# A four-part graph network on one core: set-up without table round trips, a first layer on full-width rows, and work of the second layer moved into its edge loop

## Chip, cores and metric

The kernel is written in Bass for one NeuronCore of a Trainium2 chip, with the instruction stream and the semaphores of each engine written out by hand. The metric is device time in microseconds (us) of one execution. TensorE is called PE, VectorE DVE, ScalarE ACT, GpSimd POOL and SyncE SP, as in the profile.

## The reference, cut to what matters

There are 6,250 nodes with 128 features and 106,250 directed edges, sorted by destination. Four graph blocks follow one another, each with a residual sum and a layer norm. The change touches the first block and what prepares it:

```python
def _sage_conv(h, src, dst, n_nodes, Wl, bl, Wr):
    msg = jnp.take(h, src, axis=0)
    agg = jax.ops.segment_sum(msg, dst, num_segments=n_nodes)
    cnt = jax.ops.segment_sum(jnp.ones_like(src, dtype=h.dtype), dst, num_segments=n_nodes)
    agg = agg / jnp.clip(cnt, 1.0)[:, None]
    return agg @ Wl + bl + h @ Wr

h = _sage_conv(x, src, dst, n, Wl0, bl0, Wr0)      # 128 -> 256
h = _batchnorm(jax.nn.relu(h), g0, b0)
h = _sage_conv(h, src, dst, n, Wl1, bl1, Wr1)      # 256 -> 256
h = _batchnorm(jax.nn.relu(h), g1, b1)
return jax.nn.relu(h @ Wp + bp)                    # 256 -> 128
```

The three later blocks (Moebius, equivariant, graph attention) read the same edges. They use a list of nodes sorted by degree, and per-edge weights and scores that the loops of the first block compute on the side.

## The kernel before, in words

Nodes are padded to 49 tiles of 128 (`TILES`), edges lie in 831 blocks of 128. A **step** is one pair of an edge block and a node tile that it reaches: 880 steps (`STEPS`), taken as 110 bodies (`BODIES`) of 8 steps (`U`).

`setup` finds, for each node, where its edges begin (`ptr`), from that the list of steps, and a sort of the nodes by degree. It goes through DRAM tables: 49 gathers of destination rows (`drow`, L336), a table `ptr_tab` written and read back, then `stepT`/`stepE` written and read back, then 14 gathers of the steps' edge rows (L343). It also splits `x` in three bf16 parts whose sum is the fp32 value and writes them as the table `x_split` (L403 to L406). At its end it ranks the nodes (L451 to L466).

`sage_layer` runs twice (layer 0, layer 1). In a step:
- POOL gathers the 128 source rows with one indirect DMA (L700), from `x_split` in layer 0 (three parts of 128 columns) or `y_split` in layer 1 (three parts of 256). There are 16 slots (`SLOTS`), so POOL can be 12 to 16 steps ahead of PE.
- DVE makes the one-hot matrix edge-to-node of four steps at once (L200, bf16), into one of two halves.
- PE multiplies rows by one-hot, three bf16 matmuls (layer 0) or six (layer 1) (L789), into a ring of four PSUM banks.
- DVE adds the bank to `agg`, which lies feature by node (L884).

In each body PE and ACT also compute edge weights of the later blocks in fp32: L798 (256 columns), L808 (two of 256), and in layer 0 L802 (128 columns) and L815 (32 columns). DVE copies small pieces (L903, L908, L913), and ACT stores and loads (L727 to L745).

When the loop of a layer ends, `agg` is scaled by the reciprocal degree (L921), multiplied by `Wl` and added to the layer's own part times `Wr` (L829, L831; 14 chunks of 448 nodes, 2 halves of features), passed through relu (L757), tallied for the batch norm (L937) and normalised (L950). Layer 0 then transposes the result back to rows and splits it in three bf16 parts (L768, L957, L770, L959), which SP writes to `y_split` (L669); POOL meanwhile scatters the sorted node list (L704, 49 scatters). Layer 1 multiplies by `Wp` and adds the bias with a one-row matmul (L844, L845), adds `x` (L962), and runs a layer norm over 7 groups of 7 tiles (L503 to L519); POOL reduces the largest degree and gathers the first sources of each node (L1009, 49 gathers). The Moebius block starts with 49 gathers (L1104).

PE, ACT and DVE run the bodies in hardware loops of four (`fours`); POOL's stream is written out in full.

## Time and profile before

| | |
|---|---|
| median of 3 runs | 7617.18 us (7613.0 to 7625.78) |
| the profiled execution: its own time | 7613.21 us |
| its span, first to last instruction | 7611.2 us |
| granted TensorE clock, mean | 0.632 of full |
| set-up, until the first gather of layer 0 | 326.7 us |
| gathers of layer 0, first to last start | 326.7 to 1462.0 us |
| gathers of layer 1, first to last start | 1594.9 to 2709.3 us |
| first gather of the Moebius block | 2981.5 us |

A row of the timeline gives start, duration, engine, line, operation, what is written and read, and in brackets how long the engine had been idle and what released it. An fp32 matmul shows as two instructions ("x2"), each with a weight load of its own (engine PEld). "issue" is time in which the engine waited for nothing that the profile shows. The granted clock has two levels here, 0.5 (1.2 GHz) and 1.0 (2.4 GHz); a value between is a mean over time.

### The profile page before, as it was taken

Reading aid. Unit: us, or ns where it says so; the run is one execution under the profiler, and the core shown is the slowest. Engines: PE = TensorE matmul, PEld = TensorE weight load, DVE = VectorE, ACT = ScalarE, POOL = GpSimd, SP = SyncE. Lnnn points to the kernel's source line nnn. Section 1 sums busy time; section 2 is a strip of 40 time slices with the busy share of each in tenths; the row PEclk is TensorE's granted clock in tenths of the full one; section 3 lists DMA queues with packets and bytes.
Section 4 is the critical chain, followed back from the end, with each engine's and each line's share of the span. In section 5 each row is a group of like instructions: output and inputs, shape, how many; then the busy total and the mean of one; then the engine's idle time right before and its main releaser. Section 6 shows DMA issues by size and latency. Waiting matters only on the chain. (4 is left out here: it accounts for less than half of the span.)

```text
span 7611.2 us, 86798 instructions
## 1 busy us (share of the span) xinstructions
PE 2675.4 (35%) x13121; PEld 1768.7 (23%) x13121; DVE 4112.7 (54%) x10643; ACT 1491.7 (20%) x5205; POOL 5148.9 (68%) x5017
## 2 busy tenths in 40 slices
PE   0466666756677673000000005666667100000000
PEld 0244444435455442000000003333335100000000
DVE  5344443454444433676677866777777414444465
ACT  0000000120000010121222104777774000000000
POOL 3277777757777742777777564777774477777765
PEclk9666555667777775555555557788878555555555
DMA  2544444356666621222222113333332322222211
GB/s 36 101 126 123 126 123 125 88 171 198 197 198 198 195 62 45 49 46 48 48 47 48 35 26 95 101 101 101 101 101 56 84 55 52 52 52 52 53 39 32
DMA packets 433517, 681.95 MB, mean 90 GB/s; under 512 B 159150, under 2 KB 266608, under 8 KB 433120
## 3 DMA queue, kind: packets, MB, share of 16 engines
q0 software_dynamic: 203280, 470.84, 24.5%
q10 hardware_dynamic: 127152, 159.46, 6.3%
q1 hardware_dynamic: 102944, 50.32, 2.9%
q14 instruction: 120, 0.98, 0.0%
q8 instruction: 21, 0.34, 0.0%
HBM read 584.78 MB, written 95.44 MB: 89 GB/s over the span
## 5 line engine op out<-in xcount | busy, mean ns | idle before, releaser
L1116 POOL DMA_INDIRECT mb_rows<-x_tab,mb_idx x906 | 1009.1, 1114 | 342.5 <-issue 276.4
L789 PE MATMUL ps<-onehot,rows 128*128 128x128 bf16 x7920 | 945.4, 272 | 732.7 <-DMA rows<-x_split,srcS 329.5
L884 DVE TENSOR_TENSOR agg<-agg,ps 128x128 f32 (+1 forms) x1760 | 623.7, 354 | 954.6 <-PE ps L789 806.3
L1414 POOL DMA_INDIRECT eq_frow<-f_tab,srcS x880 | 894.6, 1017 | 356.8 <-issue 267.9
L1732 POOL DMA_INDIRECT gt_rows<-h_tab,gt_idx x906 | 931.8, 1028 | 298.7 <-issue 273.9
L700 POOL DMA_INDIRECT rows<-x_split,srcS x880 | 864.8, 983 | 379.3 <-issue 244.9
L700 POOL DMA_INDIRECT rows<-y_split,srcS x880 | 840.6, 955 | 333.2 <-issue 245.8
L1436 ACT ACTIVATE eq_pb<-eq_wrow 128x64 f32<-128x64 f32 (+1 forms) x3520 | 864.1, 334 | 430.9 <-DVE eq_msg L1553 366.7
L1476 PE MATMUL eq_ps<-eq_msg,eq_onehot 128*128 128x320 f32 x1760 | 739.6, 581 | 435.2 <-DVE eq_onehot L200 423.8
L789 PEld LDWEIGHTS ps<-onehot,rows 128*128 128x128 bf16 x7920 | 631.6, 120 | 1106.2 <-DVE agg L884 738.9
L1464 PE MATMUL eq_ps<-ident,eq_x 128*128 128x128 f32 x49 | 14.0, 291 | 1686.9 <-DMA eq_m<-in_L_gnn_W_l_D 1686.9
L1476 PEld LDWEIGHTS eq_ps<-eq_msg,eq_onehot 128*128 128x128 f32 x1760 | 425.9, 254 | 748.4 <-DVE eq_acc L1561 570.7
L200 DVE TENSOR_TENSOR onehot<-iota,dstS 128x512 bf16<-128x512 f32 x440 | 305.3, 694 | 275.3 <-issue 263.0
L1561 DVE TENSOR_TENSOR eq_acc<-eq_acc,eq_ps 128x320 f32 x880 | 425.0, 483 | 51.6 <-issue 29.8
L808 PE MATMUL ps<-w2d,hT 128*128 128x256 f32 x880 | 415.8, 624 | 0.0
L1464 PEld LDWEIGHTS eq_ps<-ident,eq_x 128*128 128x128 f32 x49 | 7.3, 151 | 1688.7 <-issue 1687.2
L731 ACT ACTIVATE wrow<-ps 128x512 f32<-128x512 f32 x220 | 131.3, 597 | 1268.7 <-PE ps L808 1268.7
L1845 DVE TENSOR_TENSOR gt_alpha<-gt_rows,gt_scores_in 128x196 f32<-128x196 f32 (+5 forms) x36 | 9.5, 264 | 671.5 <-DMA gt_rows<-h_tab,gt_idx 671.0
L1179 DVE TENSOR_TENSOR mb_prod<-mb_rows,mb_xd 128x256 f32<-128x256 f32 (+4 forms) x128 | 140.5, 1098 | 401.8 <-DMA mb_rows<-x_tab,mb_idx 322.3
L1153 ACT ACTIVATE mb_rows<-mb_rows,mb_gm 128x128 f32<-128x128 f32 x906 | 268.5, 386 | 361.6 <-DVE mb_gm L1222 361.6
L1009 POOL DMA_INDIRECT span_src<-in_src,span_at x147 | 161.0, 1095 | 243.3 <-DVEq L1805 158.5
L1548 DVE TENSOR_TENSOR eq_msg<-eq_pb,eq_frow 128x512 f32<-128x512 f32 x220 | 152.4, 693 | 259.5 <-DMA eq_frow<-f_tab,srcS 248.2
(395 smaller groups left out, 5021.9 us busy)
## 6 DMA issues: line engine op xcount, KB each, us to landing
eq_wrow<-w_tab ACTq DMA_DIRECT2D x223, 264.0 KB, 3.0
w_tab<-wrow ACTq DMA_DIRECT2D x220, 264.0 KB, 2.7
es<-in_side ACTq DMA_DIRECT2D x220, 136.0 KB, 2.6
mb_rows<-x_tab,mb_idx POOLq DMA_INDIRECT x906, 2.6
gt_rows<-h_tab,gt_idx POOLq DMA_INDIRECT x906, 2.5
rows<-x_split,srcS POOLq DMA_INDIRECT x880, 2.7
rows<-y_split,srcS POOLq DMA_INDIRECT x880, 3.1
eq_frow<-f_tab,srcS POOLq DMA_INDIRECT x880, 2.6
```

What stands on the lines that cost most here:

```text
L200: return dve.tensor_tensor(onehot[:, 4 * half:4 * half + 4], broadcast(s["iota"][:], four, 1), broadcast(s["dstS"][:, bass.ds(4 * b, 4)], ...
L700: pool.indirect_dma_start(rows[:, n % SLOTS, :], None, table, bass.IndirectOffsetOnAxis(ap=s["srcS"][:, n:n + 1], axis=0)).then_inc(gather ...
L789: last = pe.matmul(ps[:, u % 4, f * P:(f + 1) * P], rows[:, slot, at:at + P], onehot[:, u], start=(part == 0), stop=(part == 2))
L808: last = pe.matmul(ps[:, 7, 2 * n * P:(2 * n + 2) * P], hT[:, n * P:(n + 1) * P], w2d[:], start=True, stop=True)
L884: dve.tensor_tensor(into, into, ps[:, u % 4, 0:W].rearrange("p (k n) -> p k n", n=P), ALU.add).then_inc(added, 1)
L1116: pool.indirect_dma_start(rows[:, r, n, :], None, t["x1"], bass.IndirectOffsetOnAxis(ap=idx[:, r, n:n + 1], axis=0)).then_inc(gathered[r][ ...
L1153: act.activation(rows[:, r, n, 0:D], rows[:, r, n, 0:D], ACT.Copy, scale=gm[:, n:n + 1]).then_inc(scaled_ready, 1 if n + 1 < UPTO[p] else ...
L1414: pool.indirect_dma_start(frow[:, n % SLOTS, :], None, t["f"], bass.IndirectOffsetOnAxis(ap=s["srcS"][:, n:n + 1], axis=0)).then_inc(gathe ...
L1436: last = act.activation(pb[:, r % 2, u, f].rearrange("p c w -> p (c w)"), wrow[:, r, bass.ds(at, 1), lo:lo + 64].rearrange("p o f -> p (o ...
L1476: pe.matmul(ps[:, 4 * r + u, 0:MC], onehot[:, 4 * r + u], msg[:, r, u], start=True, stop=True).then_inc(step_done, 1)
L1561: dve.tensor_tensor(into, into, ps[:, 4 * (r % 2) + u, 0:MC], ALU.add).then_inc(added, 1)
L1732: pool.indirect_dma_start(rows[:, r, n, :], None, t["h"], bass.IndirectOffsetOnAxis(ap=idx[:, r, n:n + 1], axis=0)).then_inc(gathered[r][g ...
```

## The change

The last three quarters of the kernel are as they were. What is new:

- **Set-up.** No tables, no gathers, no split of `x`, no ranking. A new input `first` holds the destination of the first edge of each block. It is spread over the partitions; one compare with a count on DVE gives for each node tile how many blocks start before it; a bf16 one-hot product with ones gives the node tile of each step. The edge rows of the steps are then picked by 22 fp32 matmuls of 224 columns with selection matrices that DVE builds.
- **First layer** (`sage_first`). POOL gathers plain fp32 rows of `x` (512 bytes). The one-hot is fp32. PE runs two fp32 matmuls a step: one-hot by a column of ones (one column, counts degrees) and rows by one-hot (128 columns). DVE adds 129 columns. In bodies 4 to 52 PE also computes `x @ Wr + bl` of one node tile (two fp32 matmuls of 256 columns, the second with one row). After the loop: five small DVE operations for degrees, then for each of 49 node tiles one fp32 matmul (256 columns) and three DVE and two ACT operations, in node-by-feature form, without transposes and without batch norm; SP writes `y_split` and also the fp32 result before relu (`h0_tab`).
- **Second layer** (`sage_second`). Inside its edge loop: fp32 tiles of `h0_tab` are loaded and transposed (4 transposes a body, bodies 2 to 26), tallied for the first batch norm, whose scale is folded in `Wl` and `Wr`; the own part (two fp32 matmuls of 448 columns and a one-row one of 448) every second body from body 34; the ranking of the nodes in bodies 2 to 14 and 35 to 61. After the loop: the `Wl` half only; the second batch norm is folded in `Wp`; the scatters of the sorted list, the largest degree and the gathers of sources follow on POOL.
- PE, ACT and (second layer) DVE run their bodies written out, not in hardware loops.

```diff
-            sp.dma_start(xin[:], a["x"].rearrange("(t p) d -> p t d", p=P)).then_inc(x_in, 16)
...
+            sp.dma_start(first_i[:], a["first"].partition_broadcast(P)).then_inc(first_in, 16)
+            for n, name in enumerate(("src", "dst")):
+                sp.dma_start(edge_i[:, n], a[name].rearrange("(c p k) -> p c k", p=P, k=P)).then_inc(edges_in, 16)
...
+            for q in range(4):
+                pe.wait_ge(pick_ready, q + 1)
+                for n in range(2):
+                    for j, c in enumerate(chunks[q]):
+                        last = pe.matmul(ps[:, 2 + q, 256 * n:256 * n + QUART], edge_f[:, n, c], pick[q][:, j], start=(j == 0),
+                                         stop=(j == len(chunks[q]) - 1))
+                last.then_inc(picked, 1)
...
-            for i in range(TILES):
-                do(dve.tensor_scalar(junk[:], firsts[:], node_f[:, i:i + 1], 0.0, ALU.is_lt, ALU.add,
-                                     accum_out=cnt[:, i:i + 1]))
...
+                pool.indirect_dma_start(rows[:, n % SLOTS, :], None, a["x"],
+                                        bass.IndirectOffsetOnAxis(ap=s["srcS"][:, n:n + 1], axis=0)).then_inc(gathered[n % SLOTS], 16)
...
+                    pe.wait_ge(added, n + 1)
+                    pe.matmul(ps[:, u % 4, P:P + 1], onehot[:, u], s["ones"][:, 0:1], start=True, stop=True)
+                    pe.matmul(ps[:, u % 4, 0:P], rows[:, slot], onehot[:, u], start=True, stop=True).then_inc(step_done, 1)
...
+                    pe.matmul(ps[:, 5, HID:2 * HID], xT[:, n * P:(n + 1) * P], wr[:], start=True, stop=False)
+                    pe.matmul(ps[:, 5, HID:2 * HID], s["ones"][0:1, :], bl[:], start=False, stop=True).then_inc(pre_psum, 1)
...
+            for n in range(TILES + 2):
+                if n < TILES:
+                    dve.wait_ge(dense_ready, n + 1)
+                    dve.scalar_tensor_tensor(h0[:, n], ps[:, n % 4, 0:HID], rc[:, n:n + 1], h0[:, n], ALU.mult,
+                                             ALU.add).then_inc(summed, 1)
...
+                if 0 <= k - TURN < QUADS4:
+                    for m in range(key_hot(k - TURN)):
+                        do(dve.tensor_tensor(cum[:, 0], cum[:, 0], oh[:, m], ALU.add))
...
+            pool.wait_ge(rank_ready, 1)
+            for n in range(TILES):
+                pool.indirect_dma_start(t["srt"][:, :], bass.IndirectOffsetOnAxis(ap=s["rank"][:, n:n + 1], axis=0),
+                                        s["sval"][:, n, :], None).then_inc(sorted_out, 16)
...
+            order()
             for n in range(TILES):
+                dve.wait_ge(projected, n + 1)
+                dve.wait_ge(x_in[n % G], 16 * (n // G + 1))
+                do(dve.tensor_tensor(v[:, n], ps[:, n % G, 0:D], bias, ALU.add))
+                dve.scalar_tensor_tensor(v[:, n], v[:, n], 0.0, xin[:, n % G], ALU.max, ALU.add).then_inc(staged, 1)
+                if n == G:
+                    plan()
```

## Rows read from the trace of the kernel before

**Rows 1.** The page: POOL's busy tenths in 40 slices.
```profile
POOL 3277777757777742777777564777774477777765
```

**Rows 2.** Stretches: length, then each engine busy, clock, DMA share, GB/s.
```profile
326.00:1463.00 1137.00, 733.39 (x3734) 499.47 (x3734) 461.83 (x1433) 109.10 (x221) 864.82 (x880) 0.59 0.45 130
1463.00:1595.00 132.00, 75.93 (x217) 37.09 (x216) 72.04 (x142) 53.23 (x129) 58.72 (x50) 0.68 0.23 79
1595.00:2710.00 1115.00, 755.79 (x5922) 559.21 (x5922) 542.37 (x1213) 107.83 (x221) 840.27 (x880) 0.77 0.67 197
2710.00:2982.00 272.00, 180.38 (x540) 114.39 (x537) 104.03 (x384) 19.66 (x38) 47.49 (x52) 0.67 0.12 30
2982.00:7611.00 4629.00, 873.46 (x2495) 523.59 (x2495) 2785.19 (x7142) 1201.83 (x4597) 3262.95 (x3084) 0.59 0.25 61
```

**Rows 3.** Line L700: count, duration min/median/max in ns, first and last start.
```profile
L700 POOL DMA_INDIRECT rows<-x_split,srcS x880: 940/946/1462, 326.7 to 1462.0; - x176
L700 POOL DMA_INDIRECT rows<-y_split,srcS x880: 942/946/1462, 1594.9 to 2709.3; - x176
```

**Rows 4.** Groups by line, 0 to 326 us: busy, mean ns, idle before.
```profile
L396 DVE TENSOR_SCALAR_CACHE_REDUCE junk<-firsts,node_f 128x832 f32<-128x832 f32 x49 | 52.9, 1079 | 5.1 <-POOL firsts L333 3.3
...
L404 DVE TENSOR_TENSOR rest<-xin,xs 128x6272 f32<-128x6272 f32 x1 | 6.7, 6693 | 0.0
```

**Rows 5.** Timeline: fp32 matmuls and weight loads at both clocks.
```profile
355.12 1.08 PE L808 MATMUL ps<-w2d,hT 128*128 128x256 f32 x4
...
1004.93 2.02 PE L808 MATMUL ps<-w2d,hT 128*128 128x256 f32 x4
...
1011.12 0.34 PEld L802 LDWEIGHTS ps<-ea,wep 128*128 128x128 f32 x1
...
2852.90 0.76 PEld L844 LDWEIGHTS ps<-wp,agg 128*128 128x128 f32 x3
```

**Rows 6.** Timeline, both loops: a one-hot, the gather beside it, first stalls.
```profile
350.28 0.94 POOL L700 DMA_INDIRECT rows<-x_split,srcS  x1 [3.92 <-PE ps L789]
...
1011.81 0.69 DVE L200 TENSOR_TENSOR onehot<-iota,dstS 128x512 bf16<-128x512 f32 x1 [0.68 <-issue]
1012.01 1.31 POOL L700 DMA_INDIRECT rows<-x_split,srcS  x1 [0.30 <-issue]
...
1621.94 0.94 POOL L700 DMA_INDIRECT rows<-y_split,srcS  x1 [7.28 <-PE ps L789]
```

**Rows 7.** Stretches, columns as in group 2.
```profile
1475.00:1497.00 22.00, 22.00 (x57) 11.08 (x56) 8.15 (x13) 8.25 (x14) 16.72 (x18) 0.95 0.03 3
2835.00:2880.00 45.00, 45.00 (x146) 34.19 (x144) 7.00 (x24) 0.00 (x0) 0.00 (x0) 0.50 0.12 35
1530.00:1590.00 60.00, 29.86 (x94) 13.59 (x92) 37.20 (x97) 32.60 (x97) 4.94 (x6) 0.53 0.42 155
```

**Rows 8.** Timeline, the end of layer 0.
```profile
1467.25 6.69 DVE L921 TENSOR_TENSOR agg<-agg,rcb 128x6272 f32<-128x6272 f32 x1
...
1468.35 6.44 POOL L704 DMA_INDIRECT sorted_nodes<-sval,rank_i  x1 [0.30 <-issue]
...
1529.13 0.97 POOL L704 DMA_INDIRECT sorted_nodes<-sval,rank_i  x1 [0.30 <-issue]
...
1589.04 0.42 DVE L959 TENSOR_TENSOR ystage<-yrest,ystage 128x256 bf16<-128x256 f32 x1 [0.47 <-ACT ystage L770]
1589.39 0.42 DVE L957 TENSOR_TENSOR yrest<-ps,ystage 128x256 f32<-128x256 f32 x1
```

**Rows 9.** Waits, 1594 to 2710 us: total us, times, longest.
```profile
DVE agg L884 <- PE ps L789: 345.7, 456, 2.4
```

**Rows 10.** Timeline, the end of layer 1.
```profile
2815.98 1.13 DVE L937 BATCH_NORM_STATS2 stats<-agg 128x6 f32<-128x426 f32 x2 [4.86 <-ACT agg L757]
...
2907.16 0.29 DVE L962 SCALAR_TENSOR_TENSOR yT<-ps,xin 128x128 f32<-128x128 f32 x1 [1.58 <-PE ps L845]
...
2981.49 0.94 POOL L1104 DMA_INDIRECT mb_xd<-x_tab,perm  x1 [186.74 <-PEq L1043]
```

More of the change, by code:

```diff
@@ L357, in _ @@
[L357 to L368 removed]
+            pe.wait_ge(reach_ready, 1)
@@ new lines, in _ @@
+            for h in range(2):
+                last = pe.matmul(ps[:, h, 0:2 * QUART], s["ones_h"][0:TILES, :], reach[0:TILES, h * 2 * QUART:(h + 1) * 2 * QUART],
+                                 start=True, stop=True)
+            last.then_inc(counted, 1)
+            for q in range(4):
[5 more added lines that the diff above has]
+                last.then_inc(picked, 1)
@@ L474 @@
+            for q in range(4):
+                steps(q)
+            do.sync()
 class LayerNorm:
@@ new lines, in sage_second, with sb @@
+def sage_second(nc, a, t, s):
+    PAIRS = -(-TILES // 2)
+    QUADS4 = -(-TILES // 4)
+    with ExitStack() as ctx:
+        def sb(name, shape, dt=F32):
+            return ctx.enter_context(nc.sbuf_tensor(f"s1_{name}", shape, dt))
+        sem = Semaphores(nc, ctx, "s1_")
+        ps = ctx.enter_context(nc.psum_tensor("s1_ps", [P, 8, 512], F32))
+        yT = sb("yT", [P, 2, NP])
+        rcb = sb("rcb", [P, NP])
+        agg = sb("agg", [P, 2, NP])
+        rows = sb("rows", [P, SLOTS, 3 * HID], BF16)
@@ new lines, in _ @@
+                if k == CONST:
+                    pe.wait_ge(bn_ready, 1)
+                    pe.wait_ge(yT_ready, PAIRS)
+                    for f in range(2):
+                        for m in range(2):
+                            pe.matmul(ps[:, 6, f:f + 1], wr[:, m, half(f)], shift[:, m:m + 1], start=(m == 0), stop=(m == 1))
+                    for m in range(2):
+                        last = pe.matmul(ps[0:1, 6, 256:256 + HID], shift[:, m:m + 1], wl[:, m], start=(m == 0), stop=(m == 1))
+                    last.then_inc(const_psum, 1)
@@ new lines, in _ @@
+                steps(k, 4, 8)
+            pe.wait_ge(pre_ready, 2 * NCH + 1)
+            for n in range(2 * NCH):
+                c, f = n // 2, n % 2
+                if f == 0:
+                    pe.wait_ge(mean_ready, c + 1)
+                if n >= 4:
+                    pe.wait_ge(sum_ready, n - 3)
+                for k in range(2):
+                    last = pe.matmul(ps[:, n % 4, 0:CH], wl[:, k, half(f)], agg[:, k, chunk(c)], start=(k == 0), stop=(k == 1))
+                last.then_inc(dense_ready, 1)
@@ L835, in _ @@
+            pe.wait_ge(wps_ready, 1)
+            for k in range(2):
+                last = pe.matmul(ps[0:1, 7, 0:D], shift[:, k:k + 1], wp[:, k], start=(k == 0), stop=(k == 1))
+            last.then_inc(bias_psum, 1)
+            pe.wait_ge(bias_ready, 1)
+            pe.matmul(ps[:, 7, D:2 * D], s["ones"][0:1, :], bp[:], start=True, stop=True).then_inc(bias_psum, 1)
             for n in range(TILES):
@@ L846, in _ @@
-                last.then_inc(turned, 1)
+                for f in range(2):
+                    last = pe.matmul(ps[:, n % G, 0:D], yT[:, f, n * P:(n + 1) * P], wps[:, f], start=(f == 0), stop=(f == 1))
+                last.then_inc(projected, 1)
         @block.vector
         def _(dve):
+            do = Chain(dve, own)
             dve.memset(w1d[:], 0.0).then_inc(w1d_zero, 1)
             dve.memset(w2d[:], 0.0).then_inc(w1d_zero, 1)
+            dve.memset(agg[:], 0.0).then_inc(agg_zero, 1)
@@ L894, in group @@
+            one_hots(0)
+            one_hots(1)
+            dve.wait_ge(agg_zero, 1)
+            for k in range(BODIES):
+                h, i = k % BUFS, k // BUFS
                 for u in range(U):
+                    b = 2 * k + u // 4
                     if u % 4 == 0:
-                        tiles = node_tiles(dve, s, 2 * k + u // 4)
-                        if not (last and u == 4):
-                            compare(2 * k + u // 4 + 1, 1 - u // 4)
-                    add(k, u, tiles[u % 4])
+                        tiles = node_tiles(dve, s, b)
+                        if 2 <= b + 1 < 2 * BODIES:
+                            one_hots(b + 1)
+                    add(U * k + u, tiles[u % 4])
```

1192 lines of the change are left out of this document (640 added, 552 removed).

## The prediction

> **What bounds the kernel now.** I read the page first. POOL is busy in nearly every slice, the other engines are not [rows 1]. Then I cut the trace into stretches at the first and last gather of each layer [rows 2, 3]. Everything after 2982 us (4629 us of the 7611.2) runs code that the change leaves alone, so the whole question lies in the first 2982 us, in five pieces: set-up 326.7, loop of layer 0 1135.3 (1462.0 - 326.7), its end 132.9 (to 1594.9), loop of layer 1 1114.4 (to 2709.3), its end 272.2 (to 2981.49) [rows 3, 10].
>
> In both loops POOL sets the pace. A gather takes 0.946 us in the median and POOL idles 0.30 us before the next one, for nothing that the profile shows [rows 3, 6]: 1.25 us a step. 880 steps are 1100 us; the loops take 1135 and 1114. The excess is gathers that start beside a DVE operation with both inputs in SBUF: a one-hot runs until 1012.50 and the gather begun at 1012.01 takes 1.31 us [rows 6]; the extreme is a scatter of 6.44 us under the scaling of `agg`, 6.69 us [rows 8]. The three pieces around the loops are serial, and there the change can save.
>
> **The change, part by part.**
>
> *Set-up.* Gone are 49 passes of 1.08 us, four passes of the split like the one of 6.7 us shown [rows 4], 63 gathers, the table round trips and the ranking. What is left: index patterns until about 10.5 us, one pass like L396 (1.1 us) with casts and small steps until about 14.5, a product, three DVE steps of about 1 us, so that the first selection is ready at about 18.5. Then 22 fp32 matmuls of 224 columns on PE. Two of 256 columns take 2.02 us at the low clock and 1.08 at the high one [rows 5]; for 224 columns 22 matmuls are 19.4 us or 10.4. I take 14, since dense fp32 streams of 448 columns are granted the high clock (0.95 in the stretch at 1475) [rows 7]. With the copies out and the change of block, estimated at 3.5 us, the first gather comes at 36 us (bounds 30 and 42). **-291.**
>
> *Loop of layer 0.* POOL issues the same 880 gathers of 128 rows; its duration is the same for rows of 768 and 1,536 bytes [rows 3], so 512 bytes won't help it. The load moves to PE. In fp32 the weight loads follow each other by 0.21 us at the low clock: three of L844 last 0.76 us, one alone 0.34, so (0.76 - 0.34) / 2 [rows 5]. A step has two fp32 matmuls, four loads: 0.85 us (the one-column product costs as much as the other, as its loads are the same). Eight steps 6.8 us; the side work of a body by the 2.02 us of L808: L808 1.8 (less the drain), L798 0.9, L802 and L815 0.43 each, sum 10.4 us a body. In 49 of 110 bodies the own part adds 1.8 and about 0.6 for the switch to one-row weights (where L844 alternates with the one-row L845, 146 loads fill 45 us, 0.31 each and not 0.21 [rows 7]; a switch there and back is 6 x 0.10): 12.8. POOL needs 10.3 (1135.3 / 110). At the high clock PE needs half, 5.2 and 6.4. So at the low clock PE is just the slower one, at the high one it has twice the room. The clock in this loop is 0.59 now [rows 2]. With a lead of 12 to 16 gathers POOL feels only a mean over two bodies, and any stretch at 1.0 lets PE catch up twice as fast as it fell behind. I take POOL's pace plus 11 us for stretches where the lead is used up; the first stall, 3.92 us [rows 6], goes, since `agg` is cleared before the first one-hots. **+7**, bounds -35 (POOL at 1.25) and +127 (0.5 throughout: 61 x 10.4 + 49 x 12.8 = 1262).
>
> The skill speaks against this: the Trainium skill, "TensorE: Matmul & The Clock Gate", section on weight-path modes, says the fast weight load is off for fp32, and its warm-up section says that a PE kept busy is given 2.4 GHz. The trace agrees on the first (0.21 us a load); on the second it does not always: from 2835 to 2880 PE is busy 45.00 of 45 us, short fp32 matmuls with loads between, at 0.50 [rows 7]. By the page's rule the loop could not stay at PE's low-clock pace; by the row it can.
>
> DVE's adds of 129 columns instead of 128 and the fp32 one-hot cost nothing to speak of: DVE is busy 462 of 1137 us [rows 2].
>
> *End of layer 0.* From the last gather: 5.3 us until the last add (L921 starts at 1467.25 [rows 8]), up to a few us of PE's lag (4), degrees 1.5. Then per tile three DVE operations on 256 columns, which follow each other by 0.35 us (1589.04 to 1589.39 [rows 8]): 1.08 us with ends, 49 tiles 53 us; PE needs 0.5 to 1.0 a tile, ACT two operations. Filling the pipeline 2, the last stores 3.5, and the last split with the change of block 5.1 (from 1589.81 to the first gather at 1594.9 [rows 3, 8]). Sum 74.5 against 132.9: **-58**. The bound is the writing: 49 x 328 KB = 16.1 MB in 53 us is 303 GB/s. The trace has 155 GB/s at a share of 0.42 [rows 7], which scales to 369; if only 155 is had, 104 us, +49.
>
> *Loop of layer 1.* Same gathers. POOL's first stall, 7.28 us [rows 6], goes (the clearing of `agg` no longer waits for the sorted list). New on DVE: in 13 bodies a one-hot (0.69), four adds and two tallies, about 2.7 us; in 26 bodies of the ranking 1.7 to 2.1. DVE waits 345.7 us for PE in this loop [rows 9], 3.1 us a body, so it fits, narrowly. But these operations have both inputs in SBUF and hold up POOL as the one-hot does: 0.3 to 0.4 us a body in 39 bodies, 15 us. PE gets transposes and 448-column products, about 2 us a body at the low clock; it runs at 0.77 here [rows 2], and such streams are granted 1.0 [rows 7]. **+8**, bounds -10 and +120 (below). The Trainium skill, "SBUF — State Buffer", section on the two sides, names this lock; the 6.44 us scatter agrees [rows 8].
>
> *End of layer 1.* Count from the last gather, T. Adds done T+5.6; two scalings 2. 14 chunks on DVE: a scaling of 896 columns (0.96, a seventh of the 6.69 [rows 8]), two sums and two tallies of 448 (0.57 each by the 1.13 for two [rows 10]), 3.5 us with gaps, 49 us; PE has half its products left. Batch norm, folding, clearing: 8.3, T+65. Meanwhile POOL does 49 scatters at 1.27 us [rows 8], held up by the scalings: 68 us, then landing and reading back 9: T+78. This sort was hidden and is now on the path, at 13 us. Then 49 tiles at 0.75 us on DVE (two operations that wait for each other, 0.29 and the return), 37; the plan, 5; ends 1.4: T+121.4. The layer norm and the block change as before, 74 us (2907.45 to 2981.49 [rows 10]), T+195.4. POOL's 49 source gathers (61 us from the plan, T+90 on) end before it. 272.2 - 195.4: **-77.** Bounds 60 and 90.
>
> **Sum.** -291 + 7 - 58 + 8 - 77 = -411. Span 7611.2 - 411 = 7200, its run 2 us more, 7202; the median before lies 4 us above the profiled run: 7617.2 - 411 = **7206**.
>
> **Rivals.**
> - *A, the forecast*: POOL keeps the pace in both loops. 7150 to 7250. 0.57.
> - *B, PE at the low clock sets layer 0's pace*: for it, the clock of 0.59 now and 0.50 at a busy PE [rows 2, 7]; against it, any stretch at 1.0. Up to 7206 + 120 = 7326. 0.18.
> - *C, DVE sets layer 1's pace*: each of 7 side operations of a body waits half a gather (0.47) for the port: 2.7 + 3.3 - 3.1 = 2.9 us over, 39 bodies, 113 us, 7319. Against it: the one-hots are not lengthened by gathers now (0.69 [rows 6]). 0.10.
> - *D, the two tables' writing bounds the end of layer 0*: +49, 7255. 0.10.
> - *E, slower than before*: fp32 loads and products don't overlap in a stream that changes weights at each product: a step is 4 x 0.34 + 2 x 0.21 = 1.8 us, side work 6.5, 20.7 us a body, 110 bodies 2280 us: 7206 + 1138 = 8344. It decides from a body of 10.3 + 411 / 110 = 14.0 us on. Against it: the three loads of L844 in 0.76 us with products between. 0.03.
> - Better than 7150 by a faster end of either layer: 0.02.
>
> **Numbers.** A measurement here tells about 0.2% (15 us) from no change. The median of A gives 7206. The range takes in A, D, nearly all of B and C, and leaves E and the far ends: 7150 to 7325. Faster 0.96, same 0.01, slower 0.03: only E or an unseen stall costs more than 411 us.
>
> **What the profile would show.** First gather near 36 us. Layer 0's gathers 1.28 to 1.30 us apart, with PE busy over 80% and few waits of POOL for PE; B would show as waits of POOL for `ps`, with the clock near 0.5. Near 75 us between the last gather of layer 0 and the first of layer 1; D as waits for stores. In layer 1, DVE's wait for PE shrinks below 300 us and gathers over 1.0 us grow in number; C as POOL waiting for PE and PE for DVE. At the end of layer 1 about 13 us of DVE waiting for the sorted list, and the Moebius block's first gather near 195 us after the last one of layer 1. What would make me wrong most: a stretch of the clock at 0.5 through all of layer 0.

## The result, and the profile after

The changed kernel takes 7194.09 us (median of 4 runs, 7192.3 to 7197.22), the kernel before 7616.94 beside it; the ratio is 0.9444, with a 95% interval of 0.9427 to 0.946. The forecast was 7206. The profiled execution spans 7190.4 us, 420.8 less than the 7611.2 of before. Of the twelve experiments, two ran on a chip like that of this measurement (chip 6) and ten on three others, numbered 12, 0 and 1, which are alike in being some 15% slower: the kernel before took 8765, 8757 and 8722 us there. The changed kernel ran on only one of the three, chip 0 (8351 us), so what ran on chips 12 and 1 is set against another chip's run of it.

Both loops, and the first gathers of the next block, read as in [rows 3]: count, duration of a gather min/median/max in ns, first and last start.

```profile
L494 POOL DMA_INDIRECT s_rows<-in_x,srcS x880: 941/947/6499, 33.3 to 1162.8; - x176
```
```profile
L808 POOL DMA_INDIRECT s_rows<-y_split,srcS x880: 942/949/14307, 1246.9 to 2390.3; - x176
```
```profile
L1301 POOL DMA_INDIRECT mb_xd<-x_tab,perm x49: 943/947/948, 2563.3 to 2623.3; - x49
```

From these starts come the pieces. Nothing is estimated in this table; the last column but one is the measured difference to before.

| piece | before | after | forecast | measured | off by |
|---|---|---|---|---|---|
| set-up, to the first gather | 326.7 | 33.3 | -291 | -293.4 | -2 |
| loop of layer 0 | 1135.3 | 1129.5 | +7 | -5.8 | -13 |
| its end | 132.9 | 84.1 | -58 | -48.8 | +9 |
| loop of layer 1 | 1114.4 | 1143.4 | +8 | +29.0 | +21 |
| its end | 272.2 | 173.0 | -77 | -99.2 | -22 |
| the rest | 4629.7 | 4627.1 | 0 | -2.6 | -3 |
| sum | 7611.2 | 7190.4 | -411 | -420.8 | -10 |

The span was met within 10 us because errors of 9 to 22 us in four pieces (-13, +9, +21, -22) nearly cancel. That is why each piece is taken by itself below.

POOL is as full as before over the two layers, PE is now full in layer 0 (the page's busy tenths and clock tenths, and then stretches: length, busy time of each engine with instructions, clock, DMA share, GB/s; compare [rows 1, 2]):

```profile
PE   7999997667776600000000056666664000000000
...
POOL 6777774777777767777775647777771777777765
PEclk7775556778887755555555578878877555555555
```
```profile
120.00:680.00 560.00, 521.01 (x2484) 442.21 (x2482) 224.87 (x709) 70.77 (x156) 426.43 (x438) 0.71 0.36 100
680.00:1182.00 502.00, 498.06 (x2031) 468.71 (x2029) 212.09 (x648) 51.53 (x108) 368.53 (x378) 0.51 0.38 97
1182.00:1240.00 58.00, 26.85 (x72) 11.73 (x72) 44.35 (x125) 31.07 (x85) 0.00 (x0) 0.79 0.94 254
1256.00:2392.00 1136.00, 795.88 (x6309) 588.14 (x6307) 618.54 (x1475) 144.81 (x290) 867.71 (x881) 0.80 0.68 202
```

In the second half of layer 0 PE is busy 498.06 of 502 us at 0.51, the lower of its two levels (1.2 GHz). It stands at the very edge: one step more of work and it would set the pace. Who does set it can't be read from this row alone; the sum of POOL's time below and the experiments decide it.

How long gathers run tells the rest. All 880 of a loop together, by groups (busy total, mean ns, idle before and its causes): first the two loops of before, then the two of after.

```profile
L700 POOL DMA_INDIRECT rows<-x_split,srcS x880 | 864.8, 983 | 379.3 <-issue 244.9 <-POOLq L77 107.9 <-PE ps L789 26.5
```
```profile
L700 POOL DMA_INDIRECT rows<-y_split,srcS x880 | 840.6, 955 | 333.2 <-issue 245.8 <-POOLq L77 58.4 <-PE ps L789 28.9
```
```profile
L494 POOL DMA_INDIRECT s_rows<-in_x,srcS x880 | 862.4, 980 | 288.0 <-issue 275.2 <-PE s_ps L552 12.8
```
```profile
L808 POOL DMA_INDIRECT s_rows<-y_split,srcS x880 | 876.3, 996 | 351.2 <-issue 253.4 <-POOLq L77 83.2 <-PE s_ps L881 14.6
```

880 gathers at the median of 0.946 us are 832.5 us. So the time held beyond it is 32.3 us in layer 0 of before, 8.1 in layer 1 of before, 29.9 and 43.8 after. Each loop is 1099 us (879 steps of 1.25) plus what is held plus POOL's stalls: 1099 + 32.3 + 3.9 = 1135.2, 1099 + 8.1 + 7.3 = 1114.4, 1099 + 30 = 1129, 1099 + 43.8 = 1142.8. This one sum gives all four measured loops to within 1 us. In the changed kernel it needs no stall: after the first gather POOL idles 268.0 us before 879 gathers in either loop, 0.305 us each, and never over 0.31 us in layer 0 where the profile names PE.

### The profile page after: what moved, and what is told of

It reads as the page before. It is cut to its first block and busy times, and to the rows that moved or that the text cites. A ratio compares the mean times of both kernels' runs of the same rounds, so it can differ in the third digit from the quotient of the medians.

```text
span 7190.4 us, 84650 instructions
## 1 busy us (share of the span) xinstructions
PE 2870.3 (40%) x14090; PEld 2155.9 (30%) x14090; DVE 4073.3 (57%) x10736; ACT 1531.7 (21%) x5293; POOL 5103.5 (71%) x4952
## 5 line engine op out<-in xcount | busy, mean ns | idle before, releaser
L1611 POOL DMA_INDIRECT eq_frow<-f_tab,srcS x880 | 896.6, 1019 | 355.9 <-issue 268.0
L808 POOL DMA_INDIRECT s_rows<-y_split,srcS x880 | 876.3, 996 | 351.2 <-issue 253.4
L494 POOL DMA_INDIRECT s_rows<-in_x,srcS x880 | 862.4, 980 | 288.0 <-issue 275.2
L988 DVE TENSOR_TENSOR s_agg<-s_agg,s_ps 128x256 f32 x880 | 369.7, 420 | 447.3 <-PE s_ps L881 325.2
L881 PE MATMUL s_ps<-s_onehot,s_rows 128*128 128x128 bf16 x5280 | 493.8, 252 | 322.4 <-DMA s_rows<-y_split,srcS 303.7
L552 PE MATMUL s_ps<-s_onehot,s_rows 128*128 128x128 f32 x1760 | 594.3, 436 | 0.0
L881 PEld LDWEIGHTS s_ps<-s_onehot,s_rows 128*128 128x128 bf16 x5280 | 387.6, 114 | 465.1 <-DMA s_rows<-y_split,srcS 413.8
L551 PEld LDWEIGHTS s_ps<-ones,s_onehot 128*128 128x128 f32 x1760 | 417.3, 286 | 94.0 <-DMA s_rows<-in_x,srcS 62.5
L200 DVE TENSOR_TENSOR s_onehot<-iota,dstS 128x512 f32<-128x512 f32 (+1 forms) x440 | 304.9, 693 | 216.7 <-issue 159.4
L552 PEld LDWEIGHTS s_ps<-s_onehot,s_rows 128*128 128x128 f32 x1760 | 413.6, 289 | 0.0
L551 PE MATMUL s_ps<-ones,s_onehot 128*128 128x1 f32 x1760 | 363.8, 276 | 45.7 <-DMA s_rows<-in_x,srcS 44.9
```

Of the source, the lines that this page charges most:

```text
L494: pool.indirect_dma_start(rows[:, n % SLOTS, :], None, a["x"], bass.IndirectOffsetOnAxis(ap=s["srcS"][:, n:n + 1], axis=0)).then_inc(gathe ...
L551: pe.matmul(ps[:, u % 4, P:P + 1], onehot[:, u], s["ones"][:, 0:1], start=True, stop=True)
L552: pe.matmul(ps[:, u % 4, 0:P], rows[:, slot], onehot[:, u], start=True, stop=True).then_inc(step_done, 1)
L808: pool.indirect_dma_start(rows[:, n % SLOTS, :], None, t["ys"], bass.IndirectOffsetOnAxis(ap=s["srcS"][:, n:n + 1], axis=0)).then_inc(gath ...
L881: last = pe.matmul(ps[:, u % 4, half(f)], rows[:, slot, at:at + P], onehot[:, u], start=(part == 0), stop=(part == 2))
L988: dve.tensor_tensor(into, into, ps[:, n % 4, 0:HID].rearrange("p (k n) -> p k n", n=P), ALU.add).then_inc(added, 1)
```

## What held the first gathers

Before any experiment the trace of after shows two gathers of a new kind. Timeline (start, duration, idle before): the start of layer 0, then of layer 1.

```profile
33.29 1.30 POOL L494 DMA_INDIRECT s_rows<-in_x,srcS  x1 [19.95 <-issue]
...
34.70 5.33 DVE L594 MEMSET s_agg<- 128x6321 f32 x1 [1.27 <-issue]
34.89 6.50 POOL L494 DMA_INDIRECT s_rows<-in_x,srcS  x1 [0.30 <-issue]
...
39.94 1.22 DVE L200 TENSOR_TENSOR s_onehot<-iota,dstS 128x512 f32<-128x512 f32 x2
```
```profile
1246.95 14.31 POOL L808 DMA_INDIRECT s_rows<-y_split,srcS  x1 [83.20 <-POOLq L77]
...
1249.39 10.51 DVE L974 MEMSET s_agg<- 128x12544 f32 x1 [2.56 <-issue]
...
1259.82 1.22 DVE L200 TENSOR_TENSOR s_onehot<-iota,dstS 128x512 bf16<-128x512 f32 x2
```

The gather of 34.89 takes 6.50 us, the first of layer 1 14.31 us; both end 1.36 us after the clearing of `agg` beside them (34.70 + 5.33, 1249.39 + 10.51). The second began 2.44 us before its clearing did, and an unheld gather would have ended by then. Before, the clearings (5.29 and 10.51 us) ran beside three and six gathers that took 0.94 to 0.95 each and were not held. So the clearing alone can't be the cause. What differs in the code: before, DVE waited for the clearing right behind it; after, the first one-hots follow it at once.

## The experiments

**First group of runs (chip 12): who paces layer 0, and what holds gathers.** The changed kernel did not run on this chip. Its values on chip 0, from the second group, have to serve as the control; the kernel before took 8765 us on the one and 8757 on the other (`after_again`: loop of layer 0 1322.2, its end 88.0, loop of layer 1 1341.8, its end 283.7).

`count_half`, the count product in bf16:

```diff
-  pe.matmul(ps[:, u % 4, P:P + 1], onehot[:, u], s["ones"][:, 0:1], ...)
+  pe.matmul(ps[:, u % 4, P:P + 1], onehot[:, u].bitcast(BF16).rearrange("p (n h) -> p n h", h=2)[:, :, 1],
+            s["ones_h"][:, 0:1], ...)
```

> Layer 0's one-column count product reads the upper halves of the fp32 one-hot as bf16, so a step has one cheap weight load there in place of two fp32 loads (0.42 us of PE a step at the low clock). Theory A, POOL paces layer 0: its 880 gathers (1129.5 us from the first to the last) move by less than 10 us, since POOL waits for PE only 12.8 us in all; PE's busy time in 38 to 1182 us falls from 1087 to about 900; end of layer 0 some 1 to 2 us shorter; total -5 to -15 us against the changed kernel. Rival B, PE at the low clock paces the second half (498 us busy of 502 at 0.51): a body loses 8 x 0.3 us there, the gathers close up to POOL's own 1.25 us a step, 10.0 a body, and the loop falls by 20 us or more.

Measured: ratio 0.9494 (0.9469 to 0.9519), loop 1306.7, -15.5. The loop moved by more than that between chips with nothing edited in it but its first microseconds (1318.2 on chip 0 and 1299.4 on chip 1, `three_waits` and its repeat), so this is inconclusive.

`count_twice`, the same product issued twice:

```diff
+  for _ in range(2):
       pe.matmul(ps[:, u % 4, P:P + 1], onehot[:, u], s["ones"][:, 0:1], start=True, stop=True)
```

> Layer 0 does the one-column count product twice in each step (the output is unchanged, PE gets two more fp32 loads and products a step, 0.42 us at the low clock, so a body rises from about 10.2 to 13.6 us there and from 5.2 to 6.9 at the high clock). If PE stays at the low clock when it is the slower one: 110 x 13.6 = 1496 us instead of 1129.5, +367, so that most of the change's gain is gone, with the clock near 0.5 throughout. If a PE that is always busy gets the high clock, as the rule of the Trainium skill weighed in the prediction has it: POOL keeps the pace, the loop stays within 10 us of 1129.5 with the clock near 0.8 or above.

Measured: ratio 0.9756 (0.9733 to 0.9778), loop 1537.0: +215 against the control, +230 against `count_half` on the same chip. Stretches, and POOL's wait for PE from 120 to 1560 us:

```profile
120.00:680.00 560.00, 560.00 (x2401) 495.28 (x2402) 163.17 (x505) 52.43 (x116) 317.30 (x310) 0.56 0.26 70
680.00:1560.00 880.00, 880.00 (x3749) 834.98 (x3750) 266.72 (x831) 65.91 (x137) 527.42 (x512) 0.51 0.27 75
```
```profile
POOL s_rows L494 <- PE s_ps L553: 409.1, 206, 4.9
```

1537.0 / 110 is 13.97 us a body, where 10.2 + 8 x 0.42 = 13.6 was expected at the low clock. PE is busy 880.00 of 880 us and stays at 0.51, and POOL waits 409 us for it. So this is what rival B looks like, and PE's room in the changed kernel at the low clock was less than one product a step. The Trainium skill, "TensorE: Matmul & The Clock Gate", section on warm-up, would have a PE that is kept busy at 2.4 GHz; this row contradicts it for a stream of short fp32 products with a weight load each.

`half_gathers`, only the even steps gathered, the odd ones multiply the rows of the step before:

```diff
+  if n % 2:
+      continue
   pool.indirect_dma_start(rows[:, n % SLOTS, :], None, a["x"], ...)
...
-  slot = n % SLOTS
+  slot = n % SLOTS // 2 * 2
```

> Leaves work out: layer 0 gathers only the even steps, and the odd steps multiply the rows of the step before again. POOL then needs 440 x 1.25 = 550 us, so the loop shows PE's own pace (PE does all it did). Theory A' (POOL paces, and PE's low clock comes from being fed at POOL's pace): without POOL's pace the clock rises and the loop falls to 600 to 800 us. Rival B (PE in this stream runs at the low clock whatever feeds it, and its demand of 10.2 us a body happens to equal POOL's): the loop stays at 1110 to 1130 us with the clock near 0.5; then POOL was not the only bound of layer 0.

Measured, in a single run: the loop is 926.2 us, against 1322.2.

```profile
38.00:500.00 462.00, 443.79 (x2856) 388.06 (x2856) 255.38 (x827) 80.46 (x176) 263.05 (x259) 0.94 0.40 113
500.00:960.00 460.00, 460.00 (x1889) 435.73 (x1887) 185.39 (x584) 44.19 (x90) 201.33 (x181) 0.50 0.27 74
```

Neither theory has it whole. Up to near 480 us PE runs mostly at the high clock (0.94 in the first row) and a body takes 7.0 us; after that it is busy 460.00 of 460 us at 0.50, and a body takes 10.24 us (20.48 us for the sixteen steps of eight gathers). The 10.24 is PE's own pace at the low clock, the term that the prediction put at 10.4; the high-clock body is 7.0, in bodies with the own part, put at 6.4. Why the clock fell near 480 us, after 64.01 busy us of the 69 before (410 to 479), the runs don't show.

`onehot_four`, the one-hot as four operations with one tensor input each, in both layers:

```diff
-  return dve.tensor_tensor(onehot[:, 4 * half:4 * half + 4], broadcast(s["iota"][:], four, 1),
-                           broadcast(s["dstS"][:, bass.ds(4 * b, 4)], four, 2), ALU.is_equal)
+  for u in range(4):
+      last = dve.tensor_scalar(onehot[:, 4 * half + u], s["iota"][:], s["dstS"][:, ...4 * b + u...], None, ALU.is_equal)
+  return last
```

> In both layers one_hot is written as four DVE operations of 128 columns with one tensor input and a scalar per partition, in place of one of 512 columns with two tensor inputs. Theory, a gather that starts beside a two-input operation is held until it ends (7 gathers over 1.0 us in 10 bodies of layer 0, each some 0.36 us over): no held gathers are left in layer 0, whose loop falls from 1129.5 to 1100 to 1110, and layer 1's from 1143.4 by 15 to 25 (its side work still holds some). Rival, what holds the gather is any DVE operation on SBUF: as many or more gathers over 1.0 us, loops unchanged or longer, by up to 20 us for DVE's longer one-hots.

Measured: ratio 0.9625 (0.9596 to 0.9655). The time that gathers are held in layer 0 falls from 22.6 us (`after_again`) to 7.9, of which 5.1 is the gather beside the clearing; in layer 1 it falls from 33.7 to 24.2, of which 12.9 is the first gather. So in the steady loop the one-input form holds almost nothing, as the theory has it. But the loop of layer 0 is 50 us longer (1372.6; 66 longer than in `count_half` on the same chip), where at most +20 was allowed, and that of layer 1 is 1349.5 against 1341.8 where 15 to 25 less was expected: the remedy costs more than it saves there, and why is open. It was not tried on the first chip. And at the clearings the theory fails:

```profile
34.89 6.02 POOL L502 DMA_INDIRECT s_rows<-in_x,srcS  x1 [0.30 <-issue]
...
39.92 1.53 DVE L207 TENSOR_SCALAR s_onehot<-iota,dstS 128x128 f32<-128x128 f32 x8
```
```profile
1502.97 13.84 POOL L816 DMA_INDIRECT s_rows<-y_split,srcS  x1 [96.13 <-POOLq L77]
...
1505.40 10.51 DVE L982 MEMSET s_agg<- 128x12544 f32 x1 [2.56 <-issue]
...
1515.83 1.53 DVE L207 TENSOR_SCALAR s_onehot<-iota,dstS 128x128 bf16<-128x128 f32 x8
```

Eight one-hots with one tensor input stand behind each clearing, and the gathers take 6.02 and 13.84 us, nearly as long as with the two-input form.

**Second group (chip 0): three waits.** With the changed kernel as control on the same chip.

> The changed kernel itself, so that the three beside it can be set against it on the same chip. Expected 7194 us (0.944 of the kernel before) on a chip like that of the first measurement; in the session of the single edits the kernel before took 8765 us, and if this one is as slow, about 0.95.

Measured: 8351.19 us, ratio 0.9544 (0.9515 to 0.9573).

`three_waits` makes three edits in stretches that follow one another:

```diff
 # both layers, DVE: clearing behind the one-hots, after four gathers
-  dve.memset(agg[:], 0.0).then_inc(agg_zero, 1)
   compare(0)
   compare(1)
+  dve.wait_ge(issued, 1)
+  dve.memset(agg[:], 0.0).then_inc(agg_zero, 1)
 # end of layer 0: rc turned on PE, copied by ACT, stored as 49 rows
-  sp.dma_start(t["rc"].rearrange("(t p o) -> p t o", p=P, o=1), rc[:].unsqueeze(2), ...)
+  pe.transpose(ps[0:TILES, 4, 0:P], rc[:], s["ident"][:])
+  act.copy(rcT[:], ps[0:TILES, 4, 0:P])
+  sp.dma_start(t["rc"].rearrange("(t p) -> t p", p=P), rcT[:])
 # end of layer 1: order() at tile 26, plan() at tile 33, SP's load of the sorted list ahead of tile 24's rows
-  order()
   for n in range(TILES):
+      if n == SORT + 2:
+          order()
```

> Three edits of the changed kernel in stretches that follow one another, so each is read in its own stretch. First, in both layers the one-hots come ahead of the clearing of agg, which starts once POOL has issued four gathers. Theory: what held the second gather of layer 0 for 6.50 us and the first of layer 1 for 14.31 us is the clearing that starts beside it; gathers 1 to 16 all take about 0.95 us, layer 0 loses 5.6 us and layer 1 up to 13.4. Rival: a clearing of agg holds whichever gather runs beside it, so the fifth or sixth gather takes 6.5 and 11.5 us instead and nothing is gained. Second, rc is turned on PE and stored as 49 rows of 512 bytes instead of 6272 elements of 4 bytes. Theory: the element store keeps the DMA engines busy in 1171 to 1195 us, so ACT's 17 us wait for the first y_split store (DVE's 16.1 us behind it) vanishes and the end of layer 0 falls from 84.1 to about 68. Rival: the wait is for the volume of the table stores (227 to 254 GB/s), and it only comes a few tiles later: 80 to 84. Third, DVE projects 26 of the 49 tiles before it waits for the sorted list. Theory: the 13.7 us wait is covered, end of layer 1 173 falls to about 159. Rival: POOL's source gathers, which now start no earlier, end last, gain under 8. In all -45 to -50 us, or 7147.

Measured: 8301.09 us, ratio 0.9488 (0.9466 to 0.951); set against 0.9544, the intervals don't overlap. In the profiled runs 38 of the 70 us between the two lie in the unedited rest of the kernel, so each edit is read from its own stretch.

The stores. The end of layer 0 falls from 88.0 to 73.8. In the trace of after the cause is plain. Timeline, and the issue with its size and the us until it landed:

```profile
1170.76 0.38 SPq L468 DMA_DIRECT2D rc_tab<-s_rc  x1
...
1173.67 22.86 SPq L473 DMA_DIRECT2D y_split<-s_ystage  x7
...
1194.97 0.42 ACT L532 ACTIVATE s_ystage<-s_h 128x256 bf16<-128x256 f32 x1 [16.98 <-DMA y_split<-s_ystage]
...
1195.42 0.43 DVE L668 SCALAR_TENSOR_TENSOR s_yrest<-s_h,s_ystage 128x256 f32<-128x256 f32 x1 [16.07 <-ACT s_ystage L532]
```
```profile
rc_tab<-s_rc SPq DMA_DIRECT2D x1, 24.5 KB, 23.8
```

SP's store of `rc` (6272 elements of 4 bytes) goes out at 1170.76 and lands 23.8 us later. The first table store is issued behind it at 1173.67; ACT, which wants its buffer back, gets it at 1194.97 and has waited 16.98 us for it, DVE 16.07 behind ACT. In `three_waits` neither wait is there. The rival, that the volume bounds, falls: once the element store is through, the tables are written at 254 GB/s (1182 to 1240, the first 13 us of it still waiting) and the tiles follow at DVE's pace of 1.06 us.

The clearing. In layer 1 nine gathers beside it take 0.94 or 0.95 us each, none is held. In layer 0 one is, and only in the middle of the clearing:

```profile
35.34 0.43 SPq L461 DMA_DIRECT2D s_atte<-in_L_gnn_att_edge  x1
...
36.15 5.33 DVE L616 MEMSET s_agg<- 128x6321 f32 x1 [1.27 <-issue]
36.28 0.94 POOL L496 DMA_INDIRECT s_rows<-in_x,srcS  x1 [0.30 <-issue]
...
37.53 0.94 POOL L496 DMA_INDIRECT s_rows<-in_x,srcS  x1 [0.30 <-issue]
...
38.78 3.65 POOL L496 DMA_INDIRECT s_rows<-in_x,srcS  x1 [0.30 <-issue]
...
41.39 0.23 DVE L619 TENSOR_TENSOR s_wedge<-s_wedge,s_atte 128x128 f32<-128x128 f32 x1
```

The gathers of 36.28 and 37.53 run freely beside the clearing begun at 36.15; that of 38.78 is held for 3.65 us. The operation that DVE does next is L619 with two tensor inputs, whose second input `atte` was sent for at 35.34. This formed a new theory: POOL is held by a two-input operation that already stands issued behind the clearing, for as long as it stands there. The part on standing behind fits: before, a wait on the clearing kept the one-hots back; in layer 1 of this kernel, too. The part on two inputs doesn't: the one-input one-hots of `onehot_four` hold as well. Nor does every operation hold that stands behind a clearing. In the kernel before, a cast follows the clearing of another tile with no wait between, and no gather is held:

```profile
1602.08 2.59 DVE L871 MEMSET span_src<- 128x3038 int32 x1 [0.59 <-issue]
...
1602.46 0.95 POOL L700 DMA_INDIRECT rows<-y_split,srcS  x1 [0.30 <-issue]
...
1604.59 0.12 DVE L872 CAST sdeg<-sback 128x49 f32<-128x49 int32 x1
```

Which property of an operation decides is open.

The sort. The end of layer 1 falls from 283.7 to 278.5 only, on a chip where that piece is 111 us longer than on the first; the last group has it on a chip like the first.

`three_and_onehot` adds the one-input form to all selections of both layers, `all_four` the bf16 count besides.

> The three edits, and every is_equal selection of the two layers as DVE operations of 128 columns with one tensor input (four for each one-hot). Theory from the session of the single edits, where gathers over 1.0 us fell from about 90 to 24 in layer 0: the time that gathers spend held (30 us over 880 gathers in layer 0, 30 in layer 1 without its first gather) falls to 5 and 10, so each loop is 20 to 25 us shorter than with the three edits, near 1100, as long as PE follows. Rival: PE at the low clock, which had 498 us of work in 502, becomes the pace of layer 0's second half (10.2 us a body), so that layer 0 gains less than 8 us and POOL waits for PE; layer 1 gains its 20.

> As the kernel before it in this list, and the one-column count product reads the upper halves of the one-hot as bf16, which takes about 0.3 us a step off PE at the low clock (8 to 9 us a body instead of 10.2). If POOL paces layer 0 once PE has that room: loop of layer 0 at 1105 or below (10.0 us a body), POOL waiting for PE less than 5 us, total 7095 to 7110. If layer 0 was not limited by PE in the kernel before it either: no difference between the two above 5 us.

Measured: 0.9595 (0.9569 to 0.9621) and 0.9627 (0.9593 to 0.9661). Held time in layer 0 is 3.1 and 3.5 us, the loop 1372.4 and 1415.0 against 1318.2 in `three_waits`; layer 1's is 1342.3 and 1342.6 against 1333.7. Both expectations missed: with the holds gone the loops are longer. In layer 0 the added time is POOL's idle time (489.0 us in `three_waits`, then 558.5 and 600.3), and the profile puts most of it to waits for PE (125.2, 227.3, 333.3). PE's load is not the reason, since `all_four` has the smallest load and the longest loop; what is stays open.

**Third group (chip 1), two repeats.**

> The same kernel as three_waits, in another session. On the chip of the two sessions of edits the engines stop between instructions for nothing that the profile shows (PE 359 us in 1000 us of layer 0, 41 or less on the first chip), and the end of layer 1 took 284 us instead of 173. On a chip like that of the first measurement: first gather of layer 1 near 1 us, end of layer 0 near 68 to 70, end of layer 1 near 159, total 7140 to 7150, a ratio of 0.938. On the slow chip again: a repeat of 0.949.

> The same kernel as all_four, in another session. Theory: the 53 us that it lost in layer 0 on the slow chip come from its larger number of DVE instructions on a chip that delivers them late. On a chip like that of the first measurement the held gathers are gone (under 6 us of hold in each loop) and both loops are near 1105 us; total 7095 to 7110. Rival: four short operations that follow each other in DVE cost the time themselves, by delaying the adds and so PE; then layer 0 is at 1130 or above there too.

Measured: 0.9466 (0.9433 to 0.9499) and 0.9579 (0.954 to 0.9618). It repeats: the end of layer 0 is 79.1 and 76.1, and the loop of layer 0 is again longer with one-input selections, 1362.3 against 1299.4. Whether that would be so on the first chip stayed open.

**Fourth group (chip 6, like the first: the kernel before 7602.34).** `clear_wait` tests the part on standing behind with one line in each layer; the clearing itself stays where it was:

```diff
   dve.memset(agg[:], 0.0).then_inc(agg_zero, 1)
+  dve.wait_ge(agg_zero, 1)
```

> The changed kernel with one line more in each layer: DVE waits for the clearing of agg right behind it, ahead of the first one-hots. The clearing itself starts at the same moment beside the same gathers. Theory, formed after three_waits (ten gathers beside the clearing of layer 1 were not held, one of layer 0 was, from the time at which DVE's next two-input operation had its inputs): what holds POOL is not the clearing but the two-input operation that already stands issued behind it. Then the second gather of layer 0 takes 0.95 us instead of 6.50 and the first of layer 1 about 1 us instead of 14.31, and the two loops are shorter by up to 5.6 and 13.4 us; total 0.2% less, near the limit of what the times can tell. Rival: the clearing holds the gathers that start with it, whatever follows; then 6.5 and 14.3 us stay.

Measured: 7172.88 us, ratio 0.9432 (0.9419 to 0.9445), which overlaps with that of the changed kernel, so the times don't decide and the timeline does:

```profile
35.15 5.33 DVE L594 MEMSET s_agg<- 128x6321 f32 x1 [1.27 <-issue]
35.34 0.95 POOL L494 DMA_INDIRECT s_rows<-in_x,srcS  x1 [0.30 <-issue]
```
```profile
1238.61 0.94 POOL L809 DMA_INDIRECT s_rows<-y_split,srcS  x1 [83.13 <-POOLq L77]
...
1241.05 10.51 DVE L975 MEMSET s_agg<- 128x12544 f32 x1 [2.56 <-issue]
1241.11 0.94 POOL L809 DMA_INDIRECT s_rows<-y_split,srcS  x1 [0.30 <-issue]
...
1251.89 1.29 DVE L200 TENSOR_TENSOR s_onehot<-iota,dstS 128x512 bf16<-128x512 f32 x2 [0.33 <-DVE s_agg L975]
```

The clearings take 5.33 and 10.51 us as before and start at the same place. The gather begun 0.19 us after the first takes 0.95 instead of 6.50; the first of layer 1 takes 0.94 instead of 14.31, and so does, to 0.01, each of the nine that start beside the second clearing. The rival is out: what stands behind the clearing holds, not the clearing. That it must have two inputs this run can't show, since the wait keeps everything back. The loops are 1120.8 and 1133.3, 8.7 and 10.1 shorter; 5.6 and 13.4 of that are the two gathers, the rest is other held time, 3 us either way. The Trainium skill, "SBUF — State Buffer", section on the two sides, describes a lock between DVE and POOL that an operation holds from its start to its end. That a gather is held already while the operation waits behind another only these rows show; whether it is the same lock they don't.

`best` has the wait behind the clearing, the turned `rc`, the covered sort and the bf16 count.

> The wait behind the clearing, rc turned and stored as rows, 24 tiles projected before the sorted list is waited for, and the count product from the upper halves of the one-hot. The sum of the single readings on this chip: -13 and up to -5 for the clearings, -9 to -14 for the end of layer 0, -5 for the end of layer 1, -15 for layer 0's loop: 45 to 50 us below the changed kernel's 8351 there, 0.949 of the kernel before; on a chip like that of the first measurement -50 to -55, 7140, 0.938. Rival: the loops move by 20 us from session to session whatever is edited, and hide part of it.

Measured: 7151.77 us, ratio 0.9409 (0.9396 to 0.9422), below the 0.9427 at which the changed kernel's interval begins: the fastest of all, 42 us below the changed kernel in medians (the kernel before ran 15 us faster beside it, so about 27 by the ratio: 0.0035 x 7617 = 27). Expected were 7140 and 0.938; the 15 us that the lighter count was to take off layer 0's loop didn't come. Pieces: 32.7, loop 1127.2, end 68.5, loop 1121.7, end 165.4.

```profile
120.00:680.00 560.00, 447.82 (x2036) 337.82 (x2036) 225.29 (x711) 70.27 (x154) 427.05 (x437) 0.73 0.36 99
680.00:1160.00 480.00, 358.71 (x1595) 280.40 (x1594) 191.52 (x610) 45.46 (x93) 365.45 (x376) 0.68 0.36 100
```
```profile
DVE s_agg L1168 <- DMA s_hin<-in_x: 3.7, 1, 3.7
```

This settles who paces layer 0. PE's work in the second half falls from 498.06 of 502 to 358.71 of 480 us, its clock is 0.68 instead of 0.51, and the loop does not shorten: 1127.2 beside 1120.8 with the full load (`clear_wait`). The 6.4 us between them are held time, 27.8 against 21.5, so the sum closes here too: 1099 + 27.8 = 1126.8. POOL paces it, in the changed kernel too. The end of layer 0 lost 15.6 us with the element store. The cover of the sort brought 7.6 of its 13.7, since DVE now waits 3.7 us for a tile of `x` that SP issues behind the sorted list, and the next block starts 2.8 later behind its last operation; the expectation's rival had the size, but not this reason.

## Why the prediction was right, and where its terms were off

**Set-up, -291, measured -293.4.** Right as a whole. The matmuls take 10.04 us (20.80 to 30.84) where 14 were taken; the first selection is ready at 20.7 and not 18.5, as the index patterns begin at 11.96; copies and block change took 2.45 of the 3.5.

**Loop of layer 0, +7, measured -5.8.** The mechanism, POOL's pace, is right, and `best` shows it. The term that failed is "plus 11 us for stretches where the lead is used up": POOL waits 12.8 us for PE in 42 places, but each within the 0.30 us that it idles anyway (0.306 at most), so it cost nothing. The stall of 3.92 went, as said, and 2.3 of held time. A new hold of 5.6, inside that held time, was not foreseen. PE per body at the low clock: forecast 10.4, measured 10.24. The forecast had PE "just the slower one" at the low clock; it came out just the faster one, 10.24 beside POOL's 10.27 (1129.5 / 110), and that was luck: on chip 12 `count_twice` shows +215 us for 3.4 us of PE more a body.

**End of layer 0, -58, measured -48.8.** The tiles follow each other by 1.06 us (forecast 1.08). Missed was the store of `rc`: set-up had it before, under cover; now it stands in SP's queue ahead of the tables. It cost DVE a wait of 16.1 us. The other terms were 6.5 too large (PE's lag 1 us and not 4, filling and tiles 53 and not 55, the last stores and the block change 7.0 and not 8.6). Rival D named the right place, but its reason, the volume, is wrong: with `rc` stored as rows the stall is gone and the piece is 68.5.

**Loop of layer 1, +8, measured +29.0.** The stall of 7.28 went. "15 us of port holds in 39 bodies" was mis-sized and misplaced: held time grew from 8.1 to 43.8. 13.4 of it is the first gather, held by the one-hot behind the clearing, and 22.3 more than before is spread over all bodies. By what DVE is doing as each long gather begins: of the 98 gathers over 1.0 us one is the first; 83 start beside an old one-hot (24.8 us of hold) and 14 beside operations of the ranking (3.6 us, most of it beside the two-input ones L993 and L1068). None of the 279 that start beside an add is over 1.0, though the forecast counted the new adds and tallies among the operations that hold. So mostly it is not the new work that holds POOL; the old one-hots, beside which 50 gathers of this loop began before (26 of them long), now have 100 beside them. What shifts them is not shown. Rival C doesn't occur: DVE still waits 322.8 us for PE, and POOL never longer than 0.3 us.

**End of layer 1, -77, measured -99.2.** The chain was right step by step: last add at T+5.6, DVE free at T+63 (forecast T+65), sorted list at T+76.7 (T+78), a wait of 13.7 us (13). Two terms were too large. A tile takes 0.53 us and not 0.75, 11 us in 49 tiles. And "the layer norm and the block change as before, 74 us" was a misreading. The row of [rows 10] at 2907.16 is not the last tile; six more follow, at 1.87 us each:

```profile
2918.41 0.29 DVE L962 SCALAR_TENSOR_TENSOR yT<-ps,xin 128x128 f32<-128x128 f32 x1 [1.58 <-PE ps L845]
...
2919.91 1.26 DVE L503 BATCH_NORM_STATS2 sage_ln_stats<-yT 128x6 f32 x6 [0.24 <-DVE x1row L964]
```

From the last tile on it was 63 us, and after it is 64 (2498.93 to 2563.3). That is the other 11. The rest of the kernel, 4629.7 us or 61% of the span, was put at 0 and came at -2.6.

The bounds held this piece badly: they ran from 60 to 90 and it came at 99.

**What the profile was to show.** PE over 80% busy, few waits for it, more gathers over 1.0 us in layer 1, 13 us for the sorted list: as said. Three sizes missed: the end of layer 0, near 75, was 84.1; DVE's wait for PE in layer 1, below 300, was 322.8; the Moebius block's first gather, 195 us after the last of layer 1, came at 173.

## What to carry to other kernels

When work moves, look at every store that moves with it and ask what stands behind it in its queue: 25 KB in elements of 4 bytes held up the stores of 16 MB of tables for 17 us. Where one engine sets a steady pace, write its loop as count times step plus held time plus stalls; when the sum closes to 1 us, a change in the loop is a change in one of the three. Where an engine runs ahead of a long operation, a wait behind that operation can free another engine; that costs one line. And before a duration is taken over "as before", find the last instruction of the stretch, not a late one.

## What the runs showed of the hardware

A one-hot on DVE holds POOL's indirect gathers while it is still queued behind another DVE operation: 6.50 and 14.31 us with two tensor inputs, 6.02 and 13.84 with one (`onehot_four`), against 0.95 and 0.94 when a wait keeps it back. The clearing itself, 10.51 us long, holds none, and a cast behind a clearing of 2.59 us held none either.

In the steady loop the form matters. Beside a running two-input one-hot of 0.69 us, 83 of 100 gathers of layer 1 were held, by 0.30 us on average, and beside an add that reads one of its inputs from PSUM none of 279. With one-input selections the held time of all 880 gathers of layer 0 is 3.1 us (`three_and_onehot`), the one beside the clearing included.

PE's granted clock went against its load in this stream: 0.51 at 498 of 502 us busy, 0.53 at 470 of 480 (`clear_wait`), 0.68 at 359 of 480 (`best`), 0.51 at 880 of 880 (`count_twice`); but 0.94 at 444 of 462 in the start of `half_gathers`, so load alone doesn't explain it.

Chips 12, 0 and 1 ran every kernel some 15% slower, with gathers and adds of the same duration (0.95 and 0.29 us in the rows read) but with halts between them. Around 608 to 610 us of chip 0's run of the changed kernel DVE, ACT, PE and POOL all stand still and start again within 0.6 us (start, duration, idle before):

```profile
610.18 0.69 DVE L200 TENSOR_TENSOR s_onehot<-iota,dstS 128x512 f32<-128x512 f32 x1 [3.27 <-issue]
610.18 0.37 ACT L517 COPY s_h<-s_ps 128x256 f32<-128x256 f32 x1 [3.67 <-remote]
...
610.67 0.50 PEld L560 LDWEIGHTS s_ps<-s_es,s_w1d 128*128 128x128 f32 x2 [2.43 <-issue]
...
610.71 0.98 POOL L494 DMA_INDIRECT s_rows<-in_x,srcS  x1 [2.28 <-remote]
```

At this place the profile names nothing local that they waited for ("issue", "remote"). In layer 0 POOL's idle time there is 489.4 us where it is 288.0 on the first chip. What it is stays open. The edits with four DVE selections for one lost most there; that the added instructions are the reason is not shown.
